# A graph network's second layer: three engine programs written out for all 220 blocks in place of a loop of 20

## The chip, the cores and the metric

The kernel runs on one core of one Trainium2 chip. The metric is the device time of one execution in microseconds (us), the median of several runs. The engines named below are TensorE (PE, its weight loads PEld), VectorE (DVE), ScalarE (ACT), GpSimd (POOL) and SyncE (SP). An engine name with a q behind it (DVEq, PEldq) is that engine's sequencer: register, branch and semaphore instructions, which do not count as busy.

## The reference

Two layers of a graph network over 3125 nodes with 256 features and 50000 edges sorted by destination. The first layer computes a gated message for every edge and adds it up by destination. The second layer, where the change lies, is attention with 4 heads of 64:

```python
Q = (enh @ Wq + bq).reshape(N, H, D)      # K and V likewise
mod_k = K[src] + 0.2 * rel[:, None, :]
scores = jnp.einsum('ehd,ehd->eh', Q[dst], mod_k) / D ** 0.5
ex = jnp.exp(scores - segment_max(scores, dst)[dst])
w = ex / segment_sum(ex, dst)[dst]
agg = jax.ops.segment_sum(w[:, :, None] * V[src], dst, num_segments=N)
out = where(deg > 0, agg, V).reshape(N, H * D) @ Wo + bo
```

A residual and a layer norm follow.

## The kernel before

The edges are cut into chunks of 256 and the nodes into windows of 128. A block is one chunk against one window that it touches; there are 220 blocks (BLOCKS). For the second layer the node phase writes keys and values to a table in HBM (kv_tab). Then every block goes through these steps: SP fetches the block's row of destinations and relations (block_row), POOL gathers the keys and values of its 256 sources with two indirect DMAs (L469), DVE makes one-hot rows (one_hot_t, L957), PE transposes the keys and fetches the queries by one-hot matmul (keys_and_queries), ACT copies the keys (copy_keys, L687) and the query rows of the window (fetch_query, L681), DVE multiplies (products, L964), and PE adds the heads of a product into a row of scores (add_heads, the matmuls with adder). After ten blocks (BATCH = 10) the batch's maxima are found with scans on DVE (local_maxima L974, running_maxima, segment_maxima L1018), ACT takes exponents, PE turns them into columns. Seventeen steps behind its keys a block is weighted (weight_values, L1029; one_hot1, L1038), summed by PE (aggregate) and added into the window's rows (add_agg, L1060). The window number of a block is not known when the program is built; the engines load it from memory (value_load at L679, L1045, L1053).

Each engine has its own program, an ordered list of (stage, lag) that the helper `pipeline` (L274) unfolds: at step s it emits, for each stage in turn, the work of block s minus lag. With `body` = KEEP = 20 the first rounds of 20 steps are written out, as many as the largest lag needs (two here), and the steps after the last round too. What lies between is one body of 20 steps in a hardware loop (`engine.Fori`, L296), unless `straight` is set. In that loop block numbers are register values: waits compare semaphores with registers, and slices that depend on the block are addressed through registers.

```python
peeled = -(-max(lag for _, lag in stages) // body) + 1
...
if straight:
    for k in range(peeled, rounds):
        for u in range(body):
            step(k, u)
else:
    with engine.Fori(peeled, rounds) as k:
```

For DVE (largest lag 19), ACT (6) and PE (17) this gives the same split: rounds 0 and 1 written out, rounds 2 to 10 as nine passes through the loop, so eight jumps from its end back to its start, and then the remaining 19, 6 or 17 steps written out. SP's program of block rows has the same form; POOL has one written round and then its own loop of ten passes (L538). The first layer uses loops of 4 blocks (SLOTS) on these engines.

Of the kernel before, what the change touches and what calls it, by code (L numbers as in the profile page):

```python
# [19 lines left out]
BLOCKS = CHUNKS + WINDOWS - 1  # L20
# [15 lines left out]
KEEP = 2 * BATCH  # L36
# [6 lines left out]
def build(nc, x, src, dst, etype, ea, w1, wg, b_cat, w2, b2, ln0, query_col, wqkv, b_qkv, rel, wo, b_o, ln1, out):  # L43
# [12 lines left out]
    with ctx:  # L56
# [217 lines left out]
        def pipeline(engine, stages, count, body, straight=False):  # L274

            rounds = count // body

            def step(k, u):  # L280
                for stage, lag in stages:
                    if isinstance(k, int) and not 0 <= body * k + u - lag < count:
                        continue
                    stage(k + (u - lag) // body, (u - lag) % body)


            peeled = -(-max(lag for _, lag in stages) // body) + 1
            for k in range(peeled):
# [10 lines that stand above are left out]
            for u in range(max(lag for _, lag in stages)):  # L299
                step(rounds, u)  # L300
# [260 lines left out]
        def _(act):  # L561
# [149 lines left out]

            node_phase_over(act)
            act.wait_ge(q_lo_done, WINDOWS)
            pipeline(act, [(fetch_query, 0), (copy_keys, 1), (copy_scores, 2), (copy_weights, 6), (exponents, 5)], BLOCKS, KEEP)


            act.wait_ge(ow_in, 4 * 16)
# [30 lines left out]
        def _(dve):  # L748
# [302 lines left out]
            def add_agg(k, q):  # L1051
# [5 lines left out]
                else:  # L1057
# [9 lines left out]
            dve.wait_ge(segments_known, 1)  # L1067
            dve.wait_ge(agg_zero, 1)
            pipeline(dve, [(one_hot_t, 0), (products, 2), (weight_values, 17), (one_hot1, 17), (rescale, 19), (add_agg, 19), (local_maxima, 3),
                           (running_maxima, 4), (segment_maxima, 5)], BLOCKS, KEEP)  # L1070
            dve.wait_ge(agg_added, BLOCKS)


# [52 lines left out]
        def _(pe):  # L1126
# [195 lines left out]
            def aggregate(k, q):  # L1322
# [4 lines left out]
                for i in range(2):  # L1327
# [2 lines left out]

            pe.wait_ge(consts, 3)
            pipeline(pe, [(keys_and_queries, 0), (ends_of_rows, 3), (carry_to_rows, 4), (add_heads, 1), (aggregate, 17), (weights_to_columns, 5)],
                     BLOCKS, KEEP)
            pe.wait_ge(agg_added, BLOCKS)

            pe.wait_ge(bo_lo_done, 1)
# [64 lines left out]
```

## Time and profile before

| | before |
|---|---|
| median of 3 runs | 1894.05 us (1893.74 to 1898.3) |
| the profiled execution's own time | 1896.89 us |
| its span in the profile | 1895.1 us |
| PE busy | 1660.5 us (88%) |
| DVE busy | 1617.6 us (85%) |
| ACT busy | 1047.8 us (55%) |
| POOL busy | 1040.0 us (55%) |
| mean granted TensorE clock | 0.943 |

The profile covers one execution. The second layer's blocks lie between about 1029 us and 1808 us of the span. The granted clock is a share of full speed: 1.00 stands for 2.4 GHz and 0.5 for 1.2 GHz. A bracket at the end of a timeline row gives the time that the engine sat idle before the row's instruction, and what released it; "issue" means that nothing in the profile released it.

### The profile page before, as it was taken

To read this page: it belongs to the slowest core of one execution; us is meant where nothing else is said; L and a number is where in the kernel's file an instruction comes from. 1 tells how busy PE (TensorE), PEld (TensorE's weight loads), DVE (VectorE), ACT (ScalarE), POOL (GpSimd) and SP (SyncE) were. 2 spreads that over 40 slices of the span, in tenths; PEclk is the share of its full clock that TensorE was granted. 3 is DMA by queue.
4 is the path that set the end of the run, shared out by engine and by line. 5 is a ranking of instruction groups with operands and counts; after the bars stand their busy time and mean duration, and the time that the engine had idled before them with its cause. 6 is when DMAs were issued, how large, how long until landed. Compare 5 with 4: busy or idle time off the path is not lost. (4 is left out here: it accounts for less than half of the span.)

```text
span 1895.1 us, 46044 instructions
## 1 busy us (share of the span) xinstructions
PE 1660.5 (88%) x11647; PEld 1543.2 (81%) x11647; DVE 1617.6 (85%) x3652; ACT 1047.8 (55%) x2325; POOL 1040.0 (55%) x1079
## 2 busy tenths in 40 slices
PE   6979999999999999996096999889899899899844
PEld 3779999999999999996085888788788788788633
DVE  5569999999999999999874799888888788888887
ACT  1468888888888888885453444343343343343114
POOL 0056666666566666665714766565565565565164
PEclk6989999999999999998598999999999999999978
DMA  4466666666666666662227877576576576676513
GB/s 130 153 188 186 185 188 185 185 186 184 188 185 185 186 183 188 184 186 85 98 97 248 251 205 213 169 208 185 170 208 179 170 207 181 178 200 190 195 51 102
DMA packets 165698, 333.74 MB, mean 176 GB/s; under 512 B 31015, under 2 KB 101384, under 8 KB 165092
## 3 DMA queue, kind: packets, MB, share of 16 engines
q0 software_dynamic: 70400, 231.64, 42.6%
q1 hardware_dynamic: 95204, 101.16, 16.9%
q14 instruction: 74, 0.61, 0.1%
q8 instruction: 20, 0.33, 0.1%
HBM read 307.63 MB, written 25.06 MB: 176 GB/s over the span
## 5 line engine op out<-in xcount | busy, mean ns | idle before, releaser
L456 POOL DMA_INDIRECT gath<-edge_in_tab,idx x440 | 464.2, 1055 | 301.3 <-DVE gate_in L864 230.5
L469 POOL DMA_INDIRECT kept_more<-kv_tab,idx x176 | 173.4, 985 | 145.4 <-DVE weighted L1029 87.1
L1128 PE MATMUL bank<-w_lo,relu_hi 128*128 128x256 f32 x880 | 249.4, 283 | 0.0
L1128 PE MATMUL bank<-w_hi,relu_lo 128*128 128x256 f32 x880 | 249.3, 283 | 0.0
L1128 PE MATMUL bank<-w_hi,relu_hi 128*128 128x256 f32 x880 | 249.3, 283 | 0.0
L1128 PE MATMUL bank<-weighted,hot 128*128 128x260 f32 x880 | 238.7, 396 | 4.4 <-DVE agg L1060 4.4
L606 ACT ACTIVATE relu_hi<-bank 128x512 fp32r<-128x512 f32 x220 | 131.7, 599 | 141.6 <-PE bank L1128 141.6
L1128 PEld LDWEIGHTS bank<-weighted,hot 128*128 128x128 f32 x880 | 172.4, 197 | 34.5 <-DVE hot L1038 6.3
L1131 PE MATMUL bank<-ident,gath 128*128 128x128 f32 x880 | 168.8, 274 | 23.9 <-DVE ea_parts L851 13.3
L469 POOL DMA_INDIRECT hs<-kv_tab,idx x132 | 141.9, 1075 | 80.5 <-DVE weighted L1029 47.9
L873 DVE TENSOR_TENSOR msg<-bank,gate 128x512 f32<-128x512 f32 x220 | 152.1, 692 | 33.3 <-PE bank L1128 17.2
L469 POOL DMA_INDIRECT xs<-kv_tab,idx x132 | 133.5, 1011 | 70.0 <-DVE weighted L1029 32.8
L1128 PEld LDWEIGHTS bank<-w_hi,relu_lo 128*128 128x128 f32 x880 | 169.2, 192 | 0.0
L1128 PEld LDWEIGHTS bank<-w_hi,relu_hi 128*128 128x128 f32 x880 | 167.6, 190 | 0.0
L1128 PEld LDWEIGHTS bank<-w_lo,relu_hi 128*128 128x128 f32 x880 | 167.4, 190 | 0.0
L681 ACT CAST q_now<-q_tab 128x512 fp32r x220 | 136.1, 619 | 48.7 <-issue 33.6
L1128 PE MATMUL bank<-ea_parts,w_edge_hi 128*128 128x256 f32 x440 | 161.4, 367 | 0.0
L878 DVE TENSOR_TENSOR msg_lo<-msg,msg_hi 128x512 fp32r<-128x512 f32 x220 | 152.3, 692 | 7.6 <-ACT msg_hi L618 0.8
L856 DVE SCALAR_TENSOR_TENSOR relu_lo<-bank,relu_hi 128x512 fp32r<-128x512 f32 x220 | 149.7, 681 | 3.7 <-ACT relu_hi L606 3.7
L864 DVE TENSOR_TENSOR gate_in<-bank,gath 128x512 f32<-128x512 f32 x220 | 149.7, 680 | 0.0
L625 ACT ACTIVATE dist<-iota_node,rel_col 128x128 f32<-128x128 f32 x440 | 149.6, 387 | 0.0
L612 ACT ACTIVATE gate<-gate_in 128x512 f32<-128x512 f32 x220 | 139.2, 632 | 0.6 <-DVE gate_in L864 0.6
(266 smaller groups left out, 5018.9 us busy)
## 6 DMA issues: line engine op xcount, KB each, us to landing
ea_in<-in_ea SPq DMA_DIRECT2D x440, 64.0 KB
block_row<-row_tab SPq DMA_DIRECT2D x440, 64.0 KB
gath<-edge_in_tab,idx POOLq DMA_INDIRECT x440
kv_tab<-qkv_row SPq DMA_DIRECT2D x26, 258.0 KB, 2.5
edge_in_tab<-node_row SPq DMA_DIRECT2D x26, 256.0 KB, 2.0
xs<-in_x SPq DMA_DIRECT2D x1, 3328.0 KB, 15.5
rows_tab<-xs SPq DMA_DIRECT2D x1, 3328.0 KB, 9.3
rows_tab<-hs SPq DMA_DIRECT2D x1, 3328.0 KB, 10.9
```

Source lines behind the costliest of these rows:

```text
L456: g.indirect_dma_start(gath[:, q, i, :], None, edge_in_tab, bass.IndirectOffsetOnAxis(ap=idx[:, half, q, i:i + 1], axis=0)).then_inc(gath_ ...
L469: g.indirect_dma_start(kept(u, 0, KVW)[:, i, :], None, kv_tab, bass.IndirectOffsetOnAxis(ap=idx1[:, half, u % BATCH, i:i + 1], axis=0)).th ...
L606: s.activation(relu_hi[:, q % 2, :], bank[q % 2][:], ACT.Relu).then_inc(relu_hi_done, 1)
L612: s.activation(gate[:, q % 2, :], gate_in[:, q % 2, :], ACT.Sigmoid).then_inc(gate_done, 1)
L625: last = s.activation(dist[:, q % 2, i, :], iota_node[:], ACT.Square, bias=rel_col[:, ds(b, 1), i], scale=-1.0)
L681: s.copy(q_now[:, q % 2, :, :].rearrange("p t f -> p (t f)"), q_tab[:, ds(w, 1), :, :].rearrange("p o t f -> p (o t f)")).then_inc(query_f ...
L856: v.scalar_tensor_tensor(relu_lo[:, q % 2, :], in0=bank[q % 2][:], scalar=0.0, in1=relu_hi[:, q % 2, :], op0=ALU.max, op1=ALU.subtract).th ...
L864: v.tensor_tensor(gate_in[:, q % 2, :].rearrange("p (i f) -> p i f", i=2), bank[2 + q % 2][:].rearrange("p (i f) -> p i f", i=2), gath[:, ...
L873: v.tensor_tensor(msg[:, q % 2, :], bank[4 + q % 2][:], gate[:, q % 2, :], ALU.mult).then_inc(msg_done, 1)
L878: v.tensor_tensor(msg_lo[:, q % 2, :, :].rearrange("p i f -> p (i f)"), msg[:, q % 2, :], msg_hi[:, q % 2, :, :].rearrange("p i f -> p (i ...
L1128: return nc.tensor.matmul(out_, lhsT=lhs, rhs=rhs, start=start, stop=stop)
L1131: return nc.tensor.matmul(out_, lhsT=in_, rhs=ident[:], is_transpose=True, start=start, stop=stop)
```

## The change

The three calls of `pipeline` for the second layer's blocks on ACT, DVE and PE get `straight=True`. Rounds 2 to 10 are emitted as 180 written-out steps. Stages, lags, their order in a step, buffers, waits and increments stay. Block numbers become constants. The programs of SP and POOL keep their loops.

```diff
@@ scalar
-            pipeline(act, [(fetch_query, 0), (copy_keys, 1), (copy_scores, 2), (copy_weights, 6), (exponents, 5)], BLOCKS, KEEP)
+            pipeline(act, [(fetch_query, 0), (copy_keys, 1), (copy_scores, 2), (copy_weights, 6), (exponents, 5)], BLOCKS, KEEP, straight=True)
@@ vector
             pipeline(dve, [(one_hot_t, 0), (products, 2), (weight_values, 17), (one_hot1, 17), (rescale, 19), (add_agg, 19), (local_maxima, 3),
-                           (running_maxima, 4), (segment_maxima, 5)], BLOCKS, KEEP)
+                           (running_maxima, 4), (segment_maxima, 5)], BLOCKS, KEEP, straight=True)
@@ tensor
             pipeline(pe, [(keys_and_queries, 0), (ends_of_rows, 3), (carry_to_rows, 4), (add_heads, 1), (aggregate, 17), (weights_to_columns, 5)],
-                     BLOCKS, KEEP)
+                     BLOCKS, KEEP, straight=True)
```

## Rows read from the trace of the kernel before

**Rows 1.** The page: busy time of each engine, and the granted clock in 40 slices.

```profile
PE 1660.5 (88%) x11647; PEld 1543.2 (81%) x11647; DVE 1617.6 (85%) x3652; ACT 1047.8 (55%) x2325; POOL 1040.0 (55%) x1079
PEclk6989999999999999998598999999999999999978
```

**Rows 2.** Windows: stretch, length, busy us of PE PEld DVE ACT POOL, clock, DMA.

```profile
200.00:550.00 350.00, 350.00 (x2974) 350.00 (x2974) 330.80 (x596) 293.67 (x695) 214.27 (x224) 1.00 0.64 185
...
1069.00:1140.00 71.00, 68.17 (x426) 61.53 (x426) 63.52 (x170) 28.64 (x53) 48.74 (x50) 1.00 0.75 216
1140.00:1202.00 62.00, 58.76 (x365) 52.82 (x364) 57.09 (x152) 24.44 (x46) 40.94 (x41) 1.00 0.70 205
1206.00:1277.40 71.40, 64.22 (x380) 57.24 (x380) 60.06 (x158) 25.63 (x48) 41.09 (x42) 0.95 0.66 187
```

**Rows 3.** Waits, 1140 to 1790 us: total us, times, longest us.

```profile
PE bank L1128 <- DVE hs L964: 29.4, 8, 4.2
DVE ht_hi L957 <- issue: 29.3, 8, 4.2
```

**Rows 4.** Critical chain, 1203 to 1212 us: start us, us, what.

```profile
1203.17 3.80 issue
...
1207.62 0.69 DVE hs L964
...
1208.36 3.81 PE bank L1128 x8
```

**Rows 5.** Loop instructions of L296, 1140 to 1272 us: ns min/median/max, first to last start.

```profile
L296 SPq COMPARE_BRANCH  x2: 45/45/45, 1190.4 to 1261.8; - x2
...
L296 ACTq COMPARE_BRANCH  x1: 54/54/54, 1201.3 to 1201.3; - x1
L296 ACTq FUSED_REGOPS  x1: 59/59/59, 1201.6 to 1201.6; - x1
...
L296 DVEq COMPARE_BRANCH  x1: 63/63/63, 1203.1 to 1203.1; - x1
L296 DVEq FUSED_REGOPS  x1: 80/80/80, 1207.0 to 1207.0; - x1
...
L296 PEldq COMPARE_BRANCH  x1: 209/209/209, 1208.6 to 1208.6; - x1
L296 PEldq FUSED_REGOPS  x1: 64/64/64, 1208.8 to 1208.8; - x1
```

**Rows 6.** PE timeline: start us, length us, instructions, idle before. One mark a batch.

```profile
1092.79 1.13 PE L1128 MATMUL bank<-kept_more,adder 128*128 128x256 f32 x4 [1.28 <-DVE kept_more L964]
...
1124.88 1.13 PE L1128 MATMUL bank<-xs,adder 128*128 128x256 f32 x4 [1.28 <-DVE xs L964]
...
1228.65 1.13 PE L1128 MATMUL bank<-kept_more,adder 128*128 128x256 f32 x4 [1.28 <-DVE kept_more L964]
...
1260.98 1.13 PE L1128 MATMUL bank<-xs,adder 128*128 128x256 f32 x4 [1.28 <-DVE xs L964]
...
1759.33 0.92 PE L1128 MATMUL bank<-xs,adder 128*128 128x256 f32 x3 [1.27 <-DVE xs L964]
```

**Rows 7.** Windows of PE alone: stretch, length, busy us, clock, DMA share, GB/s.

```profile
1208.36:1213.86 5.50, 5.50 (x19) 0.53 0.48 127
...
1216.75:1219.64 2.89, 2.89 (x21) 1.00 0.62 156
```

**Rows 8.** Instruction queues (packets, MB, share): 1069 to 1136 us, then 1206 to 1273 us.

```profile
q8 instruction: 3, 0.05, 0.3%
q14 instruction: 5, 0.04, 0.2%
...
q14 instruction: 4, 0.03, 0.2%
```

**Rows 9.** Waits, 1069 to 1202 us: total us, times, longest us.

```profile
POOL hs L469 <- DVE weighted L1029: 7.5, 5, 2.0
...
DVE agg L1060 <- issue: 0.5, 1, 0.5
```

**Rows 10.** POOL timeline behind its loop's jump near 1131 us.

```profile
1132.79 0.97 POOL L469 DMA_INDIRECT kept_more<-kv_tab,idx  x1 [0.81 <-POOL idx L462]
```

## The prediction

> **What bounds the kernel now.** I began with the page. PE and DVE are both above 85% busy, ACT and POOL at 55%, so neither of the latter can be a bound by throughput [rows 1]. The change touches the blocks of the second layer only, so I took windows there. The kernel itself holds the comparison that I want: rounds 0 and 1 of these blocks are written out already, rounds 2 to 10 run in the loop. In the written stretch 1069 to 1140 us PE is busy 68.17 of 71.00 us at a granted clock of 1.00; in one pass of the loop, 71.40 us long, it is busy 64.22 us at 0.95 [rows 2]. Something happens once a pass. The waits name it: eight times DVE's first instruction of a round (L957) stands behind "issue", 29.3 us together, and eight times PE then waits for DVE's product (L964), 29.4 us together. Eight is the number of jumps back in nine passes [rows 3]. The chain that ended last goes through it: 3.80 us of nothing, DVE's catch-up, and PE's eight matmuls in 3.81 us [rows 4].
>
> The loop instructions show whose jump it is. DVE's branch is recorded at 1203.1 us and its next register instruction at 1207.0. ACT has 0.3 us between the two, PE 0.2 us [rows 5]. So the stop is DVE's alone; ACT and PE jump almost for free.
>
> Outside the stops the pace is even. Once a batch PE waits about 1.28 us for DVE, which is late from its scans; the rest of the batch PE works without a hole at 2.89 us a step. I use this wait as a mark for each batch. The written batch from 1092.79 to 1124.88 takes 32.09 us, a looped batch without a jump, 1228.65 to 1260.98, takes 32.33 us [rows 6].
>
> **What it removes: DVE's stop at the jump.** I cost this from marks and not from the stops, because a stop has an after-effect. From 1124.88 to 1759.33 there are 18 batches in 634.45 us, with all eight jumps among them [rows 6]. At 32.33 us each, 18 take 581.9 us. So the eight jumps cost 52.5 us, 6.6 us each.
>
> The parts agree. 29.4 / 8 = 3.7 us is PE's idle time [rows 3]. After the idle time PE's clock has fallen to half: 19 matmuls take 5.50 us at 0.53, against 21 in 2.89 us at 1.00, so 2.6 us more [rows 7]. Together 6.3 of the 6.6 us. In the written stretch, where PE has only its short waits, the clock stays at 1.00 [rows 2]. So I let both parts go with the stop.
>
> What is late next when the stop has gone? The batch's own wait of 1.28 us, and it is in both paces already.
>
> **What it removes: register work.** In the loop, waits and slices go through registers. The written batch is 32.33 - 32.09 = 0.24 us shorter [rows 6]. I lay it to DVE, which is where PE waits at the end of a batch; the sum doesn't need that. Eighteen batches give 4.3 us. It rests on a single written batch, so its bounds are 0 and 4.3 us. The loads of the window number stay, since their values come from memory. On PE the register work lies under matmuls and I cost it at nothing beyond that; without this cover it would show in the 2.89 us of a step, and it doesn't. ACT waits most of the time, so I cost its part at nothing.
>
> **What it adds: instructions to fetch.** A written program never returns to instructions that it holds. In 67 us of the written stretch, 3 packets came on instruction queue q8 and 5 on q14; in 67 us of the loop none on q8 and 4 on q14 [rows 8]. Over 577 us of written steps that is about 69 packets in place of 34, some 0.5 MB more by the megabytes of the same rows. The question is only whether an engine stands still for one. Lower bound 0, upper bound 3.80 us, what DVE stood at its jump [rows 4]. The nearest row is the written stretch, where all three engines fetched at a DMA share of 0.75 [rows 2]: from 1069 to 1202 us DVE waited for "issue" at most 0.5 us at once, and that in front of a window's add, whose address needs a load [rows 9]. I take 0.
>
> The row shows 3.80 us behind DVE's branch and nothing behind packets that straight code asks for. The Trainium skill (Runtime: NRT & Kernel Launch, "Instruction fetch mechanics") has a rule for each: a jump out of the small window held on chip waits for a DMA, while the next block in sequence is fetched ahead, "mostly hidden". By it the term added is nothing, as in my sum. The same section gives PE a window of 2048 instructions and most engines 512, which speaks against the PE part of the change: by it PE's loop fitted, and writing it out buys only fetches. That q8 is silent in the loop agrees; that PE jumps in 0.2 us agrees too.
>
> **The loops that stay.** POOL and SP keep their jumps, and DVE's stop no longer covers them. They have been seen without that cover. POOL's jump near 1131 us cost 0.81 us of waiting for its own copy, with DVE in written code [rows 10], and PE showed no wait. SP jumped at 1190.4 us, 13 us ahead of DVE's stop [rows 5], and DVE met its rows in time. POOL is busy 48.74 of 71.00 us in the written stretch [rows 2] and still waits for DVE there, 7.5 us in front of one group of gathers alone [rows 9]. Nothing is moved and no wait is added.
>
> **Sum.** 52.5 + 4.3 + 0 = 56.8 us as the most, 52.5 us with the register term at 0. The profiled execution's own time is 1896.89 us, its span 1895.1 us, the median of three runs 1894.05 us, so the profiled one is 0.15% above the median and needs no scaling. I take 56 us: 1894.05 - 56 = 1838 us, 3.0% less.
>
> **Rivals.**
> - Straight code is fetched too slowly (the other side). Place: DVE, at the end of each fetched block. If each packet on q14 stopped it as the jump does, 577 / 67 x 5 = 43 packets x 3.80 = 164 us, and the time is 1894 - 57 + 164 = 2001 us. It turns the change slower from 56.8 / 43 = 1.3 us a packet. Against it: five packets in the written stretch without any such stop [rows 8, 9]. For it: only 67 us of such code have been seen, and the early stretch may have been fetched far ahead. Chance 3%.
> - Part of the gain is lost: PE stops for its new q8 packets, 577 / 67 x 3 = 26, by about 1 us each, or the gathers come late now that no stop lets them catch up, by as much. 1838 + 26 = 1864 us. Against it stands the same stretch, and POOL's waits for DVE. What speaks for it is that fetches and gathers use the same DMA engines. Chance 7%.
> - The supply sets the mean: stops only gather up time that would be lost anyway, and the 35.2 us of a mean batch (634.45 / 18) stays. 1894 us. DMA share 0.75 in the written stretch, at 32.1 us a batch, against 0.66 in the loop, says that supply can go faster [rows 2]. Chance 2%.
> - Only the branches are worth something. By the recorded durations, 63 + 54 + 209 ns a pass [rows 5], times eight, it is 2.6 us, so 1891 us: no change that can be told. This needs the 3.80 us to have another cause than the jump, and the eight times at L957 speak against that [rows 3]. Chance 2%. The Trainium skill (Advanced Engine Details and Errata, "Control Flow Timing") gives about 108 ns for a compare-and-branch; three engines and eight passes would be 2.6 us too, an estimate.
> - A gain above the sum: the batch's 1.28 us wait shrinks as well, since DVE has less to issue: half of it in 18 batches is 11 us, 1827 us. The written batch before 1092.79 us ended on the same 1.28 us, which is against it [rows 6]. Chance 3%.
>
> **How the numbers follow.** The main case has 83% and by itself 1833 to 1845: 4.3 us down to no register term on one side, a few us of small waits (0.1 us a fetch makes 7 us) on the other. The range 1830 to 1850 us takes in these bounds and the near ends of the two neighbours. A measurement of this kernel can tell 0.3%, some 6 us. Faster by more than that: main, partial and above, 0.94 with a little of the rest; within it: supply and branches, 0.03; slower: 0.03.
>
> **What would show it.** DVE's waits for "issue" at L957 and the eight PE waits of about 3.7 us gone; marks 32.1 us apart through all rounds; the granted clock 1.00 in the windows of the second layer; the loop records of DVE, ACT and PE behind 1140 us gone and those of SP and POOL still there; q8 packets every 20 us or so. The prediction is wrong if DVE or PE show holes without a releaser at even distances, which would be fetches, or if PE's transposes begin to wait for gathers.

## The result and the profile after

The changed kernel takes 1838.66 us in the median (1833.06 to 1842.24, 4 runs) beside 1894.81 us of the kernel before. The ratio is 0.9698, with a 95% interval of 0.967 to 0.9726. On another chip, in nine and five runs, the ratio came out as 0.9696 (0.9679 to 0.9712). The profiled execution took 1842.24 us, its span 1840.2 us.

The page of the changed kernel: busy time, granted clock, and the two instruction queues. They answer to [rows 1, 8].

```profile
span 1840.2 us, 44474 instructions
...
PE 1643.3 (89%) x11647; PEld 1531.2 (83%) x11647; DVE 1604.2 (87%) x3652; ACT 1047.9 (57%) x2324; POOL 1054.6 (57%) x1079
...
PEclk7889999999999999999669899999999999999877
...
q8 instruction: 45, 0.74, 0.2%
q14 instruction: 54, 0.44, 0.1%
```

The number of busy instructions hardly differs, so the work is the same. PE lost 17 us of busy time over the span. Between the marks shown below, 1124.88 to 1759.33 us before and 1127.11 to 1704.00 us after, it lost 23.5 us (575.00 to 551.53) for the same matmuls (3421 and 3420 records), and the granted clock rose from 0.96 to 1.00: these are the matmuls that ran at half clock before. Windows of the changed kernel, to be read against [rows 2]: the written stretch as it was, then three stretches of about two batches that were in the loop before.

```profile
1069.00:1140.00 71.00, 67.36 (x419) 60.39 (x418) 63.58 (x170) 28.97 (x54) 48.56 (x50) 1.00 0.75 218
1202.00:1266.00 64.00, 61.21 (x381) 55.12 (x380) 58.49 (x158) 25.64 (x48) 42.84 (x43) 1.00 0.73 209
1266.00:1330.00 64.00, 61.22 (x381) 55.14 (x380) 58.57 (x158) 25.65 (x48) 42.82 (x43) 1.00 0.71 209
1330.00:1394.00 64.00, 61.23 (x382) 55.11 (x380) 58.55 (x158) 25.65 (x48) 42.85 (x43) 1.00 0.70 208
```

The 380 matmuls of a round took 71.4 us before and take 64 us now, at a clock of 1.00. The marks of each batch, PE's wait of about 1.28 us, answer to [rows 6]:

```profile
1127.11 1.13 PE L1128 MATMUL bank<-xs,adder 128*128 128x256 f32 x4 [1.27 <-DVE xs L964]
...
1159.28 0.92 PE L1128 MATMUL bank<-kept_more,adder 128*128 128x256 f32 x3 [1.29 <-DVE kept_more L964]
...
1704.00 1.13 PE L1128 MATMUL bank<-xs,adder 128*128 128x256 f32 x4 [1.29 <-DVE xs L964]
```

From the first mark to the last there are 18 batches, as between 1124.88 and 1759.33 before: 576.89 us in place of 634.45, so 57.6 us less. The span lost 54.9 us. The difference of 2.7 us lies outside the marks: the first mark stands 2.2 us later, and behind the last mark the kernel takes 136.2 us in place of 135.8.

The waits of the changed kernel, 1140 to 1790 us, answer to [rows 3]. All "issue" waits of DVE in that stretch are these:

```profile
DVE weighted L1029 <- issue: 0.9, 2, 0.5
DVE agg L1060 <- issue: 0.3, 2, 0.2
```

L957 with its 29.3 us has gone from the list, and so has PE's wait of 29.4 us for DVE's product; no wait of PE in the blocks grew into its place. The records of the loop line L296 end, for DVE, before the second layer's blocks (ACT's last branch is at 1009.4 us, PE's at 897.9); SP's go on:

```profile
L296 SPq COMPARE_BRANCH  x87: 40/45/58, 58.4 to 1704.8; - x87
...
L296 DVEq COMPARE_BRANCH  x75: 50/56/68, 60.4 to 1013.1; - x75
```

### The profile page after: what moved, and what is told of

The parts are those of the page before. It is cut to its first block and busy times, and to the rows that moved or that the text cites. A ratio compares the mean times of both kernels' runs of the same rounds, so it can differ in the third digit from the quotient of the medians.

```text
span 1840.2 us, 44474 instructions
## 1 busy us (share of the span) xinstructions
PE 1643.3 (89%) x11647; PEld 1531.2 (83%) x11647; DVE 1604.2 (87%) x3652; ACT 1047.9 (57%) x2324; POOL 1054.6 (57%) x1079
## 5 line engine op out<-in xcount | busy, mean ns | idle before, releaser
L1128 PE MATMUL bank<-weighted,hot 128*128 128x260 f32 x880 | 233.1, 388 | 4.4 <-DVE agg L1060 4.4
L469 POOL DMA_INDIRECT kept_more<-kv_tab,idx x176 | 180.4, 1025 | 82.1 <-issue 43.0
L1128 PEld LDWEIGHTS bank<-weighted,hot 128*128 128x128 f32 x880 | 168.4, 193 | 32.9 <-DVE hot L1038 6.3
L469 POOL DMA_INDIRECT xs<-kv_tab,idx x132 | 137.4, 1041 | 63.7 <-issue 33.4
L681 ACT CAST q_now<-q_tab 128x512 fp32r x220 | 136.2, 619 | 34.4 <-issue 26.9
```

Source lines behind the costliest of these rows:

```text
L469: g.indirect_dma_start(kept(u, 0, KVW)[:, i, :], None, kv_tab, bass.IndirectOffsetOnAxis(ap=idx1[:, half, u % BATCH, i:i + 1], axis=0)).th ...
L681: s.copy(q_now[:, q % 2, :, :].rearrange("p t f -> p (t f)"), q_tab[:, ds(w, 1), :, :].rearrange("p o t f -> p (o t f)")).then_inc(query_f ...
L1128: return nc.tensor.matmul(out_, lhsT=lhs, rhs=rhs, start=start, stop=stop)
```

## The experiments

The experiments ran on four other chips, with the kernel before beside them on each. Its medians were 2048, 2036, 1899 and 2048 us. On the first, second and fourth of these chips it took 7 to 8% longer than on the chip of the prediction; only the third was like it. So kernels are compared on one chip, by their ratio to the kernel before, and the times in the expectations, which are for a chip like the first, can't be set beside times of a slow chip. The last section says what the slow chips showed.

### VectorE alone, and the other two alone

The first kernel writes out DVE's program only. The edit against the kernel before:

```diff
-                           (running_maxima, 4), (segment_maxima, 5)], BLOCKS, KEEP)
+                           (running_maxima, 4), (segment_maxima, 5)], BLOCKS, KEEP, straight=True)
```

> Only VectorE's program is written out; TensorE and ScalarE keep their loops. Theory (the gain is VectorE's stop at its jump and the slow clock behind it): the whole gain is here, 1838 us, between 1834 and 1843, with the batch marks 32.1 us apart. Rival (the loops of TensorE and ScalarE cost something of their own, their register work or their jumps of 0.2 and 0.3 us): 1845 to 1860 us. If the register work that makes a looped batch 0.24 us longer is TensorE's, about 1842 us and marks 32.3 us apart.

The second has the other two edits and leaves DVE in its loop.

> TensorE and ScalarE are written out, VectorE keeps its loop. Theory: eight stops of 3.7 us at L957 stay, the time is that of the kernel before, 1890 to 1896 us. Rival (each loop carries a share): 1850 to 1880 us. If the new instruction packets of TensorE cost anything, it is above 1896 us.

On one slow chip, DVE alone took 2013.21 us, ratio 0.9813 (0.9767 to 0.9859). TensorE and ScalarE alone took 2050.04 us, ratio 1.0002 (0.9975 to 1.0029). So the other two loops, and PE's 25 additional instruction packets, cost nothing that could be measured there; the interval is 5.5 us to either side. In the profile of this second kernel the stops are where they were, 3.8 to 4.6 us at the longest. Its waits, 1140 to 1880 us; on this chip some waits are put down to an unknown releaser ("remote"):

```profile
DVE ht_hi L957 <- issue: 16.8, 4, 4.6
DVE ht_hi L957 <- remote: 15.3, 4, 3.8
```

Four and four make the eight jumps again. Neither of the two kernels was run on a chip like the first.

### The same pair on a second chip

> The changed kernel once more, as the partner of the kernels sent with it. The kernels sent before it ran on a chip on which the kernel before took 2048 us in place of 1894, with waits that ended about 2 us after TensorE's matmuls were done, so their times can't be set beside 1838 us. On a chip like the first: 0.970 of the kernel before, 1834 to 1843 us. On one like the second: 0.97 to 0.985, since VectorE's stops lie partly under other waits there.

> Only VectorE written out, again beside the whole change on one chip. Theory: the same as the whole change within 0.3%. Rival (the register work that costs 0.24 us a batch is TensorE's): 4 us above the whole change. Rival (the other two loops have a price of their own): over 8 us above it.

The whole change took 1993.64 us, ratio 0.9793 (0.977 to 0.9817); DVE alone took 1994.59 us, ratio 0.9787 (0.9756 to 0.9818). Their medians differ by 0.05%, and each interval is 5 to 6 us to either side. Whether the last 4 us of register work are DVE's can't be told from that.

### Two jumps in place of eight

DVE's rounds 2 to 10 as three passes through a body of 60 blocks, the rest as in the changed kernel:

```diff
+            elif grouped:
+                with engine.Fori(0, (rounds - peeled) // grouped) as j:
+                    for r in range(grouped):
+                        for u in range(body):
+                            step(grouped * j + (peeled + r), u)
...
-                           (running_maxima, 4), (segment_maxima, 5)], BLOCKS, KEEP, straight=True)
+                           (running_maxima, 4), (segment_maxima, 5)], BLOCKS, KEEP, grouped=3)
```

> As the changed kernel, but VectorE's rounds 2 to 10 run as three passes through a loop of 60 blocks: two jumps in place of eight, same register work as in the loop of 20. Theory (the price is per jump, 6.6 us): 1838 + 2 x 6.6 + up to 4 for the register work = 1851 to 1856 us, and two stops of 3.5 to 4.5 us in front of L957. Rival (the loss goes with the register work or with looped code as such, not with the jump): 1885 to 1895 us. Rival (a longer body costs more at each jump, since more has to be fetched again): over 1860 us.

It took 2025.4 us, ratio 0.9882 (0.9848 to 0.9917), beside 0.9813 with no jump and 1 with eight. Two stops are left in its profile; the line is L964 here, since the edit adds seven:

```profile
DVE ht_hi L964 <- remote: 7.5, 2, 3.7
```

By jumps alone a quarter of the 35 us should remain, 8.8 us; 12.2 us remain, with an uncertainty of some 10 us (DVE's program written out spread over 15 us, this kernel over 6). That fits a price per jump, but can't tell one price from another. So looped code as such is not what costs: almost all of this kernel's second layer is looped. And 1300 recorded instructions in a pass, where the loop of 20 has 436, don't make one stop longer, 3.7 us.

### A long body in the first layer

If length is the cause, a stop can be made where there was none. The first layer's loop on DVE has 4 blocks a pass, and the trace has 63 DVE records from branch to branch. The kernels here put 40 and 20 blocks in a pass, with five rounds of 4 written out ahead of it in place of two. The edit of the first, against the changed kernel with the helper's `grouped` branch of above (the second has grouped=5):

```diff
-                     BLOCKS, SLOTS)
+                     BLOCKS, SLOTS, grouped=10, written=5)
```

> The changed kernel with a longer body in VectorE's loop of the FIRST layer: 40 blocks a pass in place of 4, five passes, four jumps, everything else as in the changed kernel. A pass of 4 blocks has 63 recorded instructions and jumps in 0.3 us; the second layer's pass of 20 blocks had 436 and stopped 3.8 us; this one has about 630. Theory (the stop comes with a body that is too long to be held): four stops of 3.5 to 4.5 us behind VectorE's branch in the first layer, 10 to 25 us more than the changed kernel. Rival (the stop had to do with the second layer, its DMA traffic or its waits): 0.3 us at each jump as with the short body, no change of the time.

> As the kernel with a first-layer body of 40 blocks on VectorE (about 630 recorded instructions a pass, four jumps, 23 us more than the changed kernel beside it), but with 20 blocks: about 315 instructions a pass, ten passes, nine jumps. Theory A (what counts is whether the body is still held when the jump comes, and 315 instructions are held): 0.3 us at each jump, no change of the time. Theory B (any body of this length is fetched again, as the second layer's 436 instructions were): nine stops of 4 to 5 us, 30 to 50 us more than the changed kernel.

Counted in their traces the bodies have 577 and 291 records, fewer than I had estimated. With 40 blocks the kernel took 2016.26 us where the changed kernel took 1993.64 on the same chip: 22.6 us for four jumps, 5.7 us each. With 20 blocks it took 1910.97 us where the changed kernel took 1838.97: 72 us for nine jumps, 8.0 us each. It is slower than the kernel before, ratio 1.0072 (1.0053 to 1.0091). Theory B holds in kind, every jump stops, but not in size: it had 30 to 50 us. The kernel's waits, 150 to 960 us:

```profile
DVE msg L880 <- issue: 53.2, 9, 6.1
...
PE bank L1135 <- DVE relu_lo L863: 48.4, 9, 5.6
```

Nine stops of 5.9 us on DVE, nine holes of 5.4 us on PE. A window of PE alone right behind the first of them:

```profile
247.41:250.90 3.49, 3.48 (x17) 0.50 0.10 20
```

What the slow clock costs can be read from PE's timeline: from the first matmul of one block with b_parts to that of the next it takes 3.53 us elsewhere, and 5.52 to 5.90 us behind the nine holes, 2.2 us more in the mean. With 5.5 us from the last matmul before a hole to the first behind it, that is 7.7 of the 8.0 us; in the second layer it was 2.6 us [rows 7]. With 4 blocks the same loop jumped in 0.3 us, and PE had no hole between 200 and 550 us [rows 2].

The fetches themselves are in the traces, as 8 KB packets on queue q14. From 150 to 960 us the kernel with 20 blocks a pass has 48 of them, the changed kernel 2:

```profile
q14 instruction: 48, 0.39, 0.2%
...
q14 instruction: 2, 0.02, 0.0%
```

In the kernel before, three came between 1202 and 1208 us, two of them before DVE went on at 1207.0 us, and six in the whole pass from 1277.8 to 1349.3 us:

```profile
q14 instruction: 3, 0.02, 1.6%
...
q14 instruction: 6, 0.05, 0.2%
```

By the packets' times DVE goes on 1.5 to 1.6 us after the second of them has landed, at each of the eight jumps. So the stop ends with a fetch.

The Trainium skill (Runtime: NRT & Kernel Launch, "Instruction fetch mechanics") says that most engines hold 512 instructions, that the next block of 256 is fetched while the current one runs, and that a jump out of the two held blocks waits for a fetch. By the 512 alone, bodies of 436 and 291 would have been held; with a block fetched ahead, the start of such a body may be gone when the jump comes. Both stopped at every jump. By the measurement, a body of 63 records is held on VectorE and one of 291 isn't; no run here moved a body against the blocks or tried a length between the two. On TensorE about 870 records a pass (380 matmuls and 380 weight loads, [rows 2], and 110 of the sequencer) are held, with a jump in 0.2 us [rows 5], which agrees with the larger window that the page gives it.

### A delay without a jump

Is the stop more than a delay? The changed kernel gets unused work on DVE at the places of the eight old jumps:

```diff
             def one_hot_t(k, q):
                 b = KEEP * k + q
+                if q == 0 and k >= 3:
+                    for i in range(6):
+                        v.tensor_reduce(out=unused[:, i, :], in_=iota_node[:].unsqueeze(1).to_broadcast([P, 4, P]), axis=AX.X, op=ALU.add)
```

> The changed kernel with six reductions that nobody uses, about 0.6 us each by their 512 elements, at the start of VectorE's rounds 3 to 10: eight delays of some 3.6 us at the places of the old jumps. Theory (the jump hurts as a delay of VectorE and through TensorE's clock, nothing else): each delay costs TensorE 3.5 us of idle time plus 2.6 us at half clock, so 1838 + 8 x 6.3 = 1889 us, 1880 to 1893, with the granted clock at 0.53 behind each. Rival (the clock fell for another reason, or the delay is taken up by the 1.28 us that each batch waits anyway): 1855 to 1870 us.

> The changed kernel with six unused reductions at the old places of the jumps again; they took 0.676 us each, 8 x 4.0 us. Theory: on a chip like the first, TensorE idles 3.5 to 4 us at each and runs at half clock behind it, 1880 to 1895 us, about the time of the kernel before. Rival (a delay alone is taken up by slack, and the jump did more than delay): 1850 us or less. On a chip like the second the theory gives at most the difference of both kernels there.

> The changed kernel with ten unused reductions at the start of VectorE's rounds 3 to 10, 8 x 6.05 us of VectorE's time at the old places of the jumps. Theory (the jump is a delay of VectorE, and TensorE's clock falls behind it; a delay of another kind does the same): TensorE idles about 6 us each time and then runs at about half clock for one step, 2.6 us more. On a chip like the first: 8 x 8.6 = 69 us more than the changed kernel, 1900 to 1912 us, ratio to the kernel before 1.002 to 1.010. On a slow chip, where six reductions cost 3 us in all: 30 to 55 us more than the changed kernel there, since the holes now are long enough for the clock. Rival (VectorE's work is taken up by slack, the jump hurts in another way): under 15 us more than the changed kernel, ratio under 0.98 on either chip.

Six reductions gave 2013.62 us, ratio 0.9818 (0.9772 to 0.9863), on the first slow chip, where DVE written out alone had 0.9813, and 1996.63 us, ratio 0.9809 (0.9786 to 0.9833), on the second, 3.0 us above the changed kernel beside it, which is within the intervals. My expectation for a chip like the first was 1889 us, and even the rival had 17 us more than the changed kernel; on these chips the theory fell for this size of delay. Two places in the second profile show why the cost is small. DVE works 3.64 us on the reductions, PE's hole is only 2.85 us, and behind it the four matmuls take 1.13 us in one case, at full clock, and 2.07 us in the other:

```profile
1280.10 1.13 PE L1132 MATMUL bank<-hs,adder 128*128 128x256 f32 x4 [2.85 <-DVE hs L968]
...
1353.75 2.07 PE L1132 MATMUL bank<-hs,adder 128*128 128x256 f32 x4 [2.85 <-DVE hs L968]
```

All of PE's waits for DVE's products (L964, there L968) rose from 58.0 us in the changed kernel's trace to 70.0 us in this one, 12 us for 29 us of reductions; the rest must lie in waits that these chips have anyway. Why only 3 of the 12 us reach the time is not shown.

Ten reductions, 6.02 us a time, gave 2036.93 us, ratio 0.994 (0.9916 to 0.9964). The changed kernel was not run on this chip. On another slow chip it had 0.9793, and DVE alone had 0.9813 on a third, so this is some 26 to 30 us more: at or just under the lower edge of what the theory expected, and above the rival's 15. Seven of the eight holes are 5.2 us long, one is 7.4, and behind all eight the four matmuls take 2.07 us, at half clock:

```profile
1293.76 2.07 PE L1132 MATMUL bank<-hs,adder 128*128 128x256 f32 x4 [5.23 <-DVE hs L968]
```

So plain work on DVE at these places makes the same holes and the same half clock, once it is long enough. On the slow chips a share of the delay is taken up: eight times 6.02 us of work and the slow clock behind it would be more than the 26 to 30 us. On a chip like the first, a delay without a jump was not run; that a jump there costs no more than its 3.7 us and the clock rests on the sum of the parts, 6.3 of 6.6 us in the second layer and 7.7 of 8.0 in the first.

### What is left: add_heads a step later

PE's wait of 1.28 us is now the largest hole. One edit against the changed kernel:

```diff
-            pipeline(pe, [..., (carry_to_rows, 4), (add_heads, 1), (aggregate, 17), ...],
+            pipeline(pe, [..., (carry_to_rows, 4), (add_heads, 2), (aggregate, 17), ...],
```

> The changed kernel with add_heads one step later on TensorE, lag 2 for 1. What is left in a written batch is TensorE's wait of 1.28 us, and one of 0.15 us, for VectorE's product behind the scans. With lag 2 the product is due about 2 us later. Theory (the wait goes and nothing takes its place): 20 batches x 1.4 us = 28 us less than the changed kernel on a chip like the first, ratio to the kernel before 0.955. Rival (the batch's scores come a step later, VectorE's first scan waits for them and hands the wait on): no gain, 0.970. On a chip like the second, where something else sets the pace, 0 to 25 us less than the changed kernel.

> The changed kernel again as partner of the kernels of this call. 0.970 of the kernel before if the chip is like the first, 0.977 to 0.982 if it is like the other two.

It took 1854.72 us, ratio 0.9782 (0.9763 to 0.98), where the changed kernel beside it took 1838.97 us, ratio 0.9696. The edit costs 16 us. The rival was right, and more came than it had named. Waits of this kernel, 1140 to 1790 us:

```profile
DVE ln_sb L974 <- ACT s_row L694: 24.9, 18, 3.0
...
PE bank L1128 <- DVE shrink L1008: 10.7, 19, 1.5
...
PE bank L1131 <- DMA kept_more<-kv_tab,idx: 8.1, 16, 1.8
...
PE bank L1131 <- DMA hs<-kv_tab,idx: 7.3, 1, 7.3
...
PE bank L1131 <- DMA xs<-kv_tab,idx: 6.4, 13, 0.9
```

The waits for the product are gone. But the scores come late, so DVE's first scan waits 1.4 us a batch; and PE meets keys that haven't landed, 21.8 us in all, where the changed kernel has no such wait of a matmul. Why the keys are late is not shown: POOL waits less for DVE's weighting than in the changed kernel (11.4 us in place of 27.9 at kept_more). The changed kernel remains the best of those run.

## Why the prediction was right

- **The bound and the place.** The stop was DVE's alone. On the slow chips, writing out DVE gives the whole gain within the intervals, and writing out PE and ACT gives none.
- **The eight jumps, 52.5 us.** Between the marks 57.6 us went. That fits 52.5 plus the register term, and the two parts of a jump, stop and slow clock, were met again in the first layer, with a longer stop (5.5 us of hole) and a slow clock of 2.2 us. The prediction took the stop to belong to the jump and named the rule of the page for it; it did not set DVE's 436 records beside the 512 of that page. That the stop comes with a long body is shown by the runs with 20 and 40 blocks in the first layer, and that it ends with a fetch by the packets in it.
- **The register work, 0 to 4.3 us.** A batch takes 576.89 / 18 = 32.05 us, 0.28 us less than the looped 32.33 us, so 5.0 us, a little above the upper bound of 4.3. The written batch that I had used, 32.09 us, was no accident. That this difference is register work is argued, not shown: no run changes the register work alone. I had taken a little less than the full term: 56 us as the sum, against 57.6 us between the marks and 56.2 us in the medians.
- **The fetches, 0.** q8 had 25 packets more, q14 20 fewer. I had said 26 more on q8 and, by 43 packets in place of 34, some 9 more on q14. The fault is in the row for the loop [rows 8]: its stretch begins at 1206 us, behind two of the packets that came in DVE's stop, so it has 4 packets where a whole pass has 6. The jumps fetched more than straight code needs. It changed nothing in the sum. Neither DVE (1.2 us of "issue" in 650 us) nor the time shows a stand for one, and the kernel with PE and ACT written out has the ratio 1.0002.
- **The loops that stay.** POOL's and SP's jumps did not show; in the blocks of the changed kernel one weight load of PE waits 0.3 us for a gather, and no matmul does. With add_heads a step later gathers do come late, 21.8 us in all.
- **Rivals.** None of them came. The one above the sum, a shrinking 1.28 us wait, is refuted by the marks, which still end on 1.27 to 1.29 us.
- **The time.** 1838 us against 1838.66 us. Some of this closeness is luck, since the runs spread from 1833 to 1842 us.

## What to carry to other kernels

When an engine stands for a few microseconds behind "issue" at even distances, look at the records of its loop branch and at how many instructions lie between two of them. On VectorE a body of 63 records jumped in 0.3 us, bodies of 291 and more stopped it for 3.7 to 5.9 us in the mean at each pass, and TensorE lost another 2.2 to 2.6 us of clock behind that; so keep a loop's body short, or write it out, and write out only the engine that stops. A short written stretch of the same steps, here the first rounds of the pipeline, was a good measure of what writing out the rest would bring.

## What the runs showed that I had not expected

- **Chips differ by 8%.** On three of five chips the kernel before took 2036 to 2048 us. One batch of the changed kernel took 36.75 us there, from 1490.77 to 1527.52 us, in place of 32.05. The critical chain of the changed kernel on the second of these chips:

```profile
1490.77 2.01 PE bank L1128 x8
...
1527.52 2.01 PE bank L1128 x8
```

  DVE's weighting (L1029) waits there for something that the trace can't name, after PE's matmuls have been recorded as done:

```profile
DVE weighted L1029 <- remote: 67.4, 37, 2.5
```

  The mean granted clock is 0.937 to 0.949 in these runs of the changed kernel and 0.949 to 0.964 on the other chips, and a matmul's mean duration is 313 ns in place of 309; neither makes 8%. The 67.4 us are part of the 155 us that the changed kernel took longer there; what ends these waits, and where the rest of the time goes, stays open. It matters for reading a gain: the same change is worth 56 to 60 us on one kind of chip and 42 us (2035.69 - 1993.64) on the other, where part of each stop probably lies under other waits.
- **The stop isn't one length.** 3.7 us in the mean in the second layer, 5.9 us in the first layer with a shorter body. The trace shows the longer one to be two stops. At the first of the nine jumps DVE's branch stands at 239.9 us, the loop's first register instruction at 242.8, and then nothing of DVE until 246.0:

```profile
L298 DVEq COMPARE_BRANCH  x1: 68/68/68, 239.9 to 239.9; - x1
L298 DVEq FUSED_REGOPS  x1: 92/92/92, 242.8 to 242.8; - x1
...
246.07 0.69 DVE L880 TENSOR_TENSOR msg<-bank,gate 128x512 f32<-128x512 f32 x1 [5.78 <-issue]
```

  All nine are like it, 2.9 to 3.3 us and 2.8 to 3.5 us, and each part ends 1.3 to 1.5 us after an 8 KB packet on q14 has landed. So DVE waits there for two packets one after the other, 2.8 to 3.5 us apart, where the second layer's two packets come 1.5 to 1.7 us apart within one stop. Why the two loops differ in this stays open, since no run moved a body.
- **Half clock isn't certain behind a hole.** The same hole of 2.85 us was followed by full clock once and by half clock once. Behind the eight holes of 5.2 us and more with ten reductions it was half clock each time.
